# A one-core graph and expert network: building the permutation table in two matrix steps, and the order of split products in the experts

## What is computed

```python
x = x + _L0_gnn_ref(_layernorm(x), adj, ...)        # five node groups, two graph convolutions each
x = x + _L0_ffn_ref(_layernorm(x), Wg, bg, W1, b1, W2, b2)
x = x + _L1_gnn_ref(_layernorm(x), adj, nodemask, W, b)
x = x + _L1_ffn_ref(_layernorm(x), ...)             # shared MLP and 4 small experts
```

```python
gate_scores = einsum('bsd,ed->bse', x, Wg) + bg      # 8 experts
topk_scores, topk_idx = top_k(gate_scores, 2)
combine = softmax weights of the two chosen experts
for e in range(8):
    h = relu(x @ W1[e].T + b1[e])                    # 128 -> 512
    y = h @ W2[e].T + b2[e]                          # 512 -> 128
    out = out + combine[..., e:e+1] * y
```

## Time and profile before

| | us |
|---|---|
| median of 3 runs | 1334.93 (1333.78 to 1335.29) |
| the profiled execution | 1336.69 |
| its span in the trace | 1334.8 |
| block 1 | 0 to about 240.5 |
| block 2 | 240.9 to about 320.9 |
| block 3 | 321.4 to about 812 |
| block 4 | about 812 to 1334.8 |

### The profile page before, as it was taken

The page is one execution under the profiler, slowest core; times in us unless marked ns, Lnnn a source line. Parts: engine busy times, 40 slices in busy tenths (PEclk is TensorE's granted clock), DMA queues, the critical chain, the costliest instruction groups (busy, mean ns, idle before and its releaser), DMA issues. The chain is left out here.

```text
span 1334.8 us, 21838 instructions
## 1 busy us (share of the span) xinstructions
PE 1193.2 (89%) x6288; PEld 870.6 (65%) x6288; DVE 1137.0 (85%) x4033; ACT 997.9 (75%) x1947; POOL 843.4 (63%) x781
## 2 busy tenths in 40 slices
PE   5889988364999999999999993499999999999998
PEld 4767757253777777777777772366666666666665
DVE  4778998897899998999999996589898988989885
ACT  3457666493999999999999993477777777777774
POOL 3345555675777777777777763676666666667630
PEclk9999975576999999999999997599999999999999
DMA  5578764400222332322222262123222322222210
GB/s 183 200 234 265 210 184 137 169 1 19 69 80 78 78 78 78 80 79 80 79 78 79 77 77 62 54 62 85 65 70 69 84 67 70 76 76 68 68 48 24
DMA packets 137642, 124.89 MB, mean 94 GB/s; under 512 B 15630, under 2 KB 117106, under 8 KB 136371
## 3 DMA queue, kind: packets, MB, share of 16 engines
q1 hardware_dynamic: 119219, 88.06, 21.4%
q0 software_dynamic: 18304, 35.44, 11.8%
HBM read 83.78 MB, written 39.67 MB: 92 GB/s over the span
## 5 line engine op out<-in xcount | busy, mean ns | idle before, releaser
L1069 POOL DMA_INDIRECT exg<-xln_scratch,eidx x284 | 315.2, 1110 | 124.3 <-issue 69.3
L1362 POOL DMA_INDIRECT yg<-expert_rows_scratch,idx x256 | 253.4, 990 | 95.2 <-issue 72.5
L1208 DVE TENSOR_TENSOR ehl<-ehr,ehh 128x512 fp32r<-128x512 f32 x284 | 194.7, 686 | 28.7 <-ACT ehh L1093 28.5
L1090 ACT ACTIVATE ehr<-p_eh,bc 128x512 f32<-128x512 f32 x284 | 195.9, 690 | 25.1 <-PE p_eh L1128 17.0
L1093 ACT ACTIVATE ehh<-ehr 128x512 fp32r<-128x512 f32 x284 | 179.6, 633 | 9.0
L1369 POOL TENSOR_TENSOR root_l<-pre_l,mhalf 128x4 f32<-128x4 f32 x64 | 66.6, 1041 | 96.9 <-DVE pre_l L1649 96.2
L1126 PE MATMUL p_ey<-ehh,wh 128*128 128x512 f32 x284 | 124.8, 439 | 1.0 <-DVE ehl L1208 0.8
L1126 PE MATMUL p_eh<-exh,wh 128*128 128x512 f32 x284 | 124.0, 437 | 1.5 <-DVE exl L1203 1.5
L1128 PE MATMUL p_eh<-exh,wl 128*128 128x512 f32 x284 | 112.6, 396 | 0.0
L1127 PE MATMUL p_eh<-exl,wh 128*128 128x512 f32 x284 | 112.2, 395 | 0.0
L1128 PE MATMUL p_ey<-ehh,wl 128*128 128x512 f32 x284 | 111.9, 394 | 0.0
(11 more groups left out here) (228 smaller groups left out, 3152.8 us busy)
## 6 DMA issues: line engine op xcount, KB each, us to landing
expert_rows_scratch<-eyo SPq DMA_DIRECT2D x71, 256.0 KB, 2.3
xtok<-in_x_tok SPq DMA_DIRECT2D x8, 1024.0 KB, 6.8
an<-in_a_t SPq DMA_DIRECT2D x16, 512.0 KB, 4.5
xln_scratch<-xl SPq DMA_DIRECT2D x16, 512.0 KB, 4.3
at<-in_a_t SPq DMA_DIRECT2D x32, 256.0 KB, 3.0
out<-outx SPq DMA_DIRECT2D x32, 256.0 KB, 2.6
wj<-in_w_grp SPq DMA_DIRECT2D x16, 321.0 KB, 4.5
exg<-xln_scratch,eidx POOLq DMA_INDIRECT x284
```

The lines of the kernel that those rows point to most:

```text
L1069: pool.indirect_dma_start(out=xg[p][:, k, :], out_offset=None, in_=xln_d, in_offset=bass.IndirectOffsetOnAxis(ap=idx[p][:, k:k + 1], axis=0))\
L1090: nc.scalar.activation(hr[c % 2][:, :], p_h[c][:, :], ACT.Relu, bias=bc[p][:, c:c + 1])\
L1208: nc.vector.tensor_tensor(hl[:, c, :], hr[c % 2][:, :], hh[:, c, :].bitcast(F32), ALU.subtract)\
L1362: pool.indirect_dma_start(out=yg[p][:, c, k, :], out_offset=None, in_=y_d, in_offset=bass.IndirectOffsetOnAxis(ap=idx[p][:, c, k:k + 1], a ...
```

## The change

It has three parts.

1. **Start of block 1.** `cf` is loaded in two pieces: the identity first, where all of `cf` was loaded, and the rest behind the loads of the second batch. POOL and PE wait for the identity alone. The softmax of the fusion weights moves on DVE from ahead of the first turn into it, behind `pre` and `nz`.
2. **Block 2.** All 128 token columns go one way, in 16 groups of 8, by two matrix steps. The 128 tokens of a column that go to one expert have positions that lie within two neighbouring columns of the table, of which one has an even number and one an odd. First step: the weights are `mt`, 32 columns wide (2 token columns x 2 parities x 8 experts), holding the token's code; the moving matrix is the one-hot `lc` of `lo`; 16 matmuls a group fill `p_rows`, 128 rows (2 x 2 x 8 x 4) by 128. Second step: ACT copies `p_rows` to `rows_`, and one matmul with a one-hot `oh` (which row goes to which of the 284 columns, made by ACT ahead of time) adds it to `p_id`. The start column of each row comes from running counts (`p_win`, `bq`, `neg_win`), eight small matmuls and a few short DVE operations. The base of an expert enters `p_rank` by a third matmul, so `posf` is gone. The one-hot of `hi` on DVE, the scatter through memory and the last addition are gone. `lo` is stored twice in a row (`lo2`), and `lc` is now written with the 128 values innermost.
3. **Block 3.** In `up` and `down` the product with the low part of the data comes last, and the wait for it stands before that matmul; the first matmul waits only for the high part.

```diff
-TA = 2
-SC = 16
-MB = (B - SC) // TB
+MB = B // TB
+AHEAD = 5
...
-                    sp.dma_start(cf[:, :], cf_d).then_inc(c_loaded, 16)
+                    sp.dma_start(cf[:, CF_ID:CF_ID + P], cf_d[:, CF_ID:CF_ID + P]).then_inc(id_loaded, 16)
                     sp.dma_start(fw[:, :], fus).then_inc(c_loaded, 16)
                     load(1)
+                    sp.dma_start(cf[:, CF_ID + P:CF_W], cf_d[:, CF_ID + P:CF_W]).then_inc(rest_loaded, 16)
...
-                    pool.wait_ge(c_loaded, 32)
+                    pool.wait_ge(id_loaded, 16)
...
+                            if t == 0:
+                                fusion()
...
-                    for t in range(SC):
-                        for k in range(2):
-                            pool.indirect_dma_start(
-                                out=tab_d, out_offset=bass.IndirectOffsetOnAxis(ap=slot[:, k, t:t + 1], axis=0),
-                                in_=idc[:, t:t + 1], in_offset=None).then_inc(scattered, 16)
...
+                    for m in range(MB):
+                        act.wait_ge(rows_done, m + 1)
                         if m >= 2:
+                            act.wait_ge(id_done, m - 1)
+                        nc.scalar.activation(rows_[m % 2][:, :], p_rows[m % 2][:, 0:P], ACT.Copy)\
+                          .then_inc(rows_ready, 1)
+                        if m + AHEAD < MB:
+                            hot(m + AHEAD)
...
                     for m in range(MB):
                         pe.wait_ge(hot_ready, m + 1)
+                        for j in range(4):
+                            for h in range(2):
+                                for k in range(2):
+                                    last = nc.tensor.matmul(p_rows[m % 2][32 * j:32 * j + 32, 0:P],
+                                                            mt[:, k, m * TB // 2 + j, h, :],
+                                                            lc[m % 2][:, k, 2 * j + h, :],
+                                                            start=(h == 0 and k == 0), stop=(h == 1 and k == 1))
+                        last.then_inc(rows_done, 1)
+                        if m >= 1:
+                            place(m - 1)
...
                         if m >= 2:
-                            dve.wait_ge(hot_used, m - 1)
+                            dve.wait_ge(rows_done, m - 1)
                         for k in range(2):
-                            nc.vector.tensor_tensor(lc[m % 2][:, k, :, :], iota_l[:, :, :],
-                                                    lo_h[:, k, TB * m:TB * m + TB].unsqueeze(1)
-                                                    .to_broadcast([P, P, TB]), ALU.is_equal)
-                        for t in range(TB - TA):
-                            b = TB * m + t
-                            for k in range(2):
-                                last = nc.vector.tensor_scalar(hh[m % 2][:, t, k, :], iota_c, hi_f[:, k, b:b + 1],
-                                                               cf[:, CF_C + b:CF_C + b + 1], ALU.is_equal, ALU.mult)
+                            last = nc.vector.tensor_tensor(
+                                lc[m % 2][:, k, :, :].rearrange("p t (a d) -> p t a d", d=2),
+                                iota.unsqueeze(1).to_broadcast([P, TB, P // 2, 2]),
+                                lo2[:, k, TB * m:TB * m + TB, :].unsqueeze(2).to_broadcast([P, TB, P // 2, 2]),
+                                ALU.is_equal)
                         last.then_inc(hot_ready, 1)
...
                     def down(j, p, c):
+                        pe.wait_ge(hh_ready, HC * j + c + 1)
+                        nc.tensor.matmul(p_y[p][:, :], wh[p][:, cols2(c)], hh[:, c, :], start=c == 0, stop=False)
+                        nc.tensor.matmul(p_y[p][:, :], wl[p][:, cols2(c)], hh[:, c, :], start=False, stop=False)
                         pe.wait_ge(hl_ready, HC * j + c + 3)
-                        last = parts(p_y[p][:, :], wh[p][:, cols2(c)], wl[p][:, cols2(c)], hh[:, c, :], hl[:, c, :],
-                                     c == 0, c == HC - 1)
+                        last = nc.tensor.matmul(p_y[p][:, :], wh[p][:, cols2(c)], hl[:, c, :],
+                                                start=False, stop=c == HC - 1)
```

More of the change, by code:

```diff
@@ new lines, in _, with distance @@
+                    for k in range(2):
+                        for h in range(2):
+                            last = nc.scalar.activation(mt[:, k, :, h, 2 * E0 * (1 - h):2 * E0 * (1 - h) + 2 * E0],
+                                                        zero, ACT.Copy, scale=0.0)
+                    last.then_inc(pad_ready, 1)
+                    def distance(m):
+                        nc.scalar.activation(gap[m % 2][:, :], ch[:, CH_H:CH_H + NCOL], ACT.Abs,
+                                             bias=neg_win[:, m:m + 1]).then_inc(gap_ready, 1)
@@ new lines, in hot @@
+                    def hot(m):
+                        act.wait_ge(gap_ready, m + 1)
+                        last = nc.scalar.activation(oh[:, m, :], gap[m % 2][:, :], ACT.Relu, scale=-1.0, bias=1.0)
+                        if m + 2 < MB:
+                            last.then_inc(gap_used, 1)
+                            act.wait_ge(gap_used, m + 1)
+                            distance(m + 2)
+                    act.wait_ge(win_ready, 1)
+                    for m in range(2):
+                        distance(m)
@@ L870, in _ @@
+                    for m in range(AHEAD):
+                        hot(m)
                     for m in range(MB):
+                        act.wait_ge(rows_done, m + 1)
                         if m >= 2:
-                            act.wait_ge(act_hot, m - 1)
-                        for t in range(TA):
-                            b = TB * m + TB - TA + t
-                            for k in range(2):
-                                last = nc.scalar.activation(gap[m % 2][:, t, k, :], ch[:, CH_H:CH_H + NCOL], ACT.Abs,
-                                                            bias=neg_hi[:, k, b:b + 1])
@@ L896, in _ @@
                     pe.wait_ge(tot_ready, 1)
-                    nc.tensor.matmul(p_cnt[:, 0:E0], ones16, tot[:, :], start=True, stop=True).then_inc(cnt_done, 1)
+                    nc.tensor.matmul(p_cnt[:, 0:E0], ones16, totx[:, 0, 0:E0], start=True, stop=True)\
+                      .then_inc(cnt_done, 1)
+                    earlier = ch[:, CH_U:CH_U + P].rearrange("p (m t) -> p t m", t=TB)
+                    for j in range(4):
+                        for h in range(2):
+                            last = nc.tensor.matmul(p_win[32 * j:32 * j + 32, :], totx[:, h, :], earlier[:, 2 * j + h, :],
+                                                    start=(h == 0), stop=(h == 1))
@@ L906, in _, with place @@
+                    def place(m):
+                        pe.wait_ge(rows_ready, m + 1)
+                        nc.tensor.matmul(p_id[:, 0:NCOL], rows_[m % 2][:, :], oh[:, m, :],
+                                         start=(m == 0), stop=(m == MB - 1)).then_inc(id_done, 1)
+                    pe.wait_ge(pad_ready, 1)
                     for m in range(MB):
                         pe.wait_ge(hot_ready, m + 1)
[L908 to L913 removed]
@@ L950, in _ @@
[L950 to L957 removed]
+                    step(nc.vector.tensor_reduce(bq[:, :], bsel[:, :], AX.X, ALU.add))
@@ new lines, in _ @@
+                    nc.vector.tensor_tensor(val[:, 1, :, :], mask[1][:, :, :], code, ALU.mult)
+                    for k in range(2):
+                        for h in range(2):
+                            b = slice(h * B // 2, (h + 1) * B // 2)
+                            if k == 0:
+                                dve.wait_ge(rank_done, h + 1)
+                            last = nc.vector.tensor_tensor(wide[:, b, :], mask[k][:, b, :], p_rank[h][:, :, :], ALU.mult)
+                        step(last)
@@ new lines, in _, with part, half_ @@
+                    step(nc.vector.tensor_copy(par[:, :, :], par_i[:, :, :]))
+                    def part(k, c, w):
+                        a = slice(c * B // 4, (c + 1) * B // 4)
+                        return [mt[:, k, a, h, 2 * E0 * h + E0 * w:2 * E0 * h + E0 * w + E0] for h in range(2)]
+                    def half_(x, k, c, h):
+                        return x[:, k, c * B // 2:(c + 1) * B // 2].rearrange("p (i h) -> p h i", h=2)[:, h, :]
+                    iota = ch[:, CH_I:CH_I + P].rearrange("p (a d) -> p a d", d=2)
```

238 lines of the change are left out of this document (118 added, 120 removed).

## The result

The changed kernel takes 1274.18 us (median of 4 runs, 1271.83 to 1278.62) against 1335.11 for the kernel before (4 runs, 1333.78 to 1338.93): ratio 0.954, 95% interval 0.952 to 0.956. That is 61 us less; 1281 was forecast, with a range of 1271 to 1300. The profiled executions are 64.9 apart (spans 1334.8 and 1269.9), since the profiled one of after lies 2.4 under the median of its four and that of before 1.6 over the median beside it.

A forecast was written before the change was run, and what follows sets the result against it. Block 1 starts as a mostly waiting chain, DVE bounds block 2, a DVE-PE chain sets block 3's turn. Gains of 1.6 + 32 + 20 = 53.6 us from the median of 1334.93 gave 1281 us, range 1271 to 1300.

The forecast's parts named there:

- Part 1, the start: Start of block 1: POOL's power starts at 8.2 to 8.5 instead of 9.99, gaining 1.6 us (0 to 2.0), kept to the block's end.
- Part 2, the preparation: Block 2 before its loop: added and removed work sum to -0.5 us, so the loop starts at 258, give or take 2.
- Part 2, the loop: Block 2's table loop: 16 groups at 1.7 us each, 27.2, plus 1.2; part of block 2's gain of 32 us.
- the price of a narrow matmul: PE in block 2's loop: 0.112 or 0.061 us each; costly but not fatal, 1300 to 1335, chance 0.04.
- the one at 1.28 a group: Block 2's best end: all groups at 1.28 us and everything hidden, a gain of 36 us.
- The second set of `mt`: Block 2's loop: interrupts DVE and adds 1.2 us.
- The tail: End of block 2, DVE from `tge` to the last step: 4.38 us as before, putting `ids` at 288.9.
- Part 3: Block 3: the low product moves behind the others, PE sets a turn of 6.42 instead of 6.71 us, gaining 20 us.
- POOL can't follow: Block 3 rival: POOL becomes the bound, part 3 gives nothing or 11 us, time 1290 to 1301; chance 0.14.
- `lc` at one element a cycle: Block 2 loop rival: a group takes 2.46 us, block 2 gains 17, time 1296; chance 0.09.
- Slower: Block 2 loop rival: narrow matmuls don't pipeline and mode changes drain PE, over 5.0 us a group, over 1335; chance 0.03.
- The lower clock: Block 2's loop: the clock stays at 1.2 GHz, time 1286, counted inside the forecast.

The follow-up runs named there:

- part3_alone: The kernel before with the changed order of the split products in block 3 alone: 1316.60 us, ratio 0.9871.
- no_part3: The changed kernel with the old order of the split products in block 3: 1293.48 us.

## Where the prediction was right and where not

**Part 1, the start: right.** 1.6 was forecast, and the runs give about 2. The power came at 8.12, a little ahead of the 8.2 to 8.5 that was said, since `cf` was there at 4.41. That block 1 keeps the gain to its end holds on average; its own swing of 232 to 241 was not in the forecast at all, though it is larger than the term. The terms of the trace with part 1 at 2 add up to 58.2 (2 + 38.9 - 2.1 + 19.7 - 0.3), so some 3 of the 61 between the medians may be this swing, and 7 of the 64.9 between the profiled executions.

**Part 2, the preparation: right.** From the first `p_tot` to the first product 16.6 us passed; 258 was 17.1 after it. POOL's power took 21.65 us and was hidden, as in the kernel before, where it took 21.25: the 12.50 of the earlier trace rows are only the part of it in that stretch.

**Part 2, the loop: wrong by 7.5 us.** Forecast were 28.4 us (16 x 1.7 + 1.2), measured 20.9 (248.80 to 269.70). The step that failed is the price of a narrow matmul: I took the row of 0.079 as a floor and the columns as the price, 1.26 to 1.8 for sixteen. The columns were right for one strip (0.107 apart at 0.50), but the sixteen go to four strips that work side by side, and the next matmul could start 0.41 after the first of them. The Trainium skill (TensorEngine Tiling (Array Packing), section Key Properties) states both that tiles run in parallel and that a change of mode drains the engine. I kept the first out of the sum; the runs bear it out, at about four times. They agree with the second too, at 0.13 to 0.18 us a change, for which a group of 1.20 had room. The form of the sum, "1.28 + 1.26 + some 0.4 of signalling for two groups", was sound: a buffer's round of filling and emptying serves two groups. With the measured 0.65 and two `lc` of 0.61 it gives (1.22 + 0.65 + 0.4) / 2 = 1.14 a group, less than DVE's own two `lc`, so DVE set it. Of the ends that I gave, the one at 1.28 a group was the right one, and the block's gain of 38.9 lies beyond even its 36. The second set of `mt` cost 2.3, not 1.2: eight operations of 0.29, which I had priced at 2.4 in the preparation and at half of it here, and DVE had no cover for them (`p_rows` 3.48 after the one before, in place of 1.20). The tail was right (4.37 for 4.38), though it began only 0.8 ahead of PE's end and not 1.9. So `ids` came 41.1 after the block's start where 48 was forecast.

**Part 3: the mechanism and the size right, the long turns left out.** The steady turn became 6.41 for a forecast 6.42, by the mechanism named: no wait for `ehl`, starts 0.23 apart. But the 19.7 came out of 0.306 x 70 = 21.4 (the middle turn went from 6.715 to 6.409) less 1.8 that longer turns took (mean over middle turn, 2.0 us before and 3.8 after), and that the forecast of 20 lies so near is in part luck: the fall of a turn was put 0.016 too small, 1.1 us in 70, and the longer turns took back 1.8. The rival's condition, that POOL can't follow, did not come: it kept up at 6.41 and even at 6.25. What did come is a thinner lead. For the middle tile rows landed 2.6 us ahead of PE before and 1.6 after, so that late ones could be felt more. The rival's price was 9 to 20; this took about 2. The 449.9 of 450 without a wait for PE could not tell: POOL shows no such wait at 6.71, at 6.41 or at 6.25.

**The start of block 3: not in the forecast.** I put it at nothing without a reason, and it is 2.1 us, of which 2.0 are the second tile's matmuls at the lower clock. `part3_alone` shows that the new order has a share in it (21.7 for 20.2), and `no_part3` that the table has one (21.0). Why the clock rises later there I can't say.

**The rivals.** `lc` at one element a cycle did not come, for the reason given (pairs side by side); taking the pair away brought it. Slower: the change of mode that it feared shows, at a fifth of a microsecond and less. The lower clock came for the whole of the table's loop and cost nothing, since DVE held it. The price of a narrow matmul was rightly named as what could break the number, but only by being higher, and it was lower. The sign was right, and so was the mechanism but for that one price. The total was 7 us too high: 6.9 more from block 2 and some 3 that are the swing of block 1, less 2.1 at the start of block 3.

## What to carry to other kernels

When two engines hand two buffers to each other, a group costs the longest of three: the one engine's work, the other's, and half of a buffer's round. Here it was DVE's own, and all rested on the price put on the other engine. Take that price from starts, one after the other, and measure it if no row has the form. When a wait is taken away from a loop whose engines are all nearly full, an engine that never waits is not thereby the bound: look at how long ahead of its consumer its data land, and lighten the suspects apart and together. And compare blocks between traces rather than ends: here a block that the change hardly touched moved by 7 us by itself, and one profiled pair would have credited it to the change.

## What the runs showed of the hardware

- Sixteen matmuls with 32-column weights and 128 moving columns take 0.44 us over four strips and 1.06 in one, at a granted clock of 1.00; 0.65 and 1.91 at 0.50. By starts they hold PE for 0.24 and 0.90, and for 0.41 and 1.71. The order (strip by strip, or changing each time) makes no difference. One strip costs as much as full width. A full-width matmul behind narrow ones starts 0.13 us later than a narrow one would at 1.00.
- An equality of two 16-bit operands, 1,024 elements on a partition, takes 0.61 us if the repeated operand lies twice in a row in memory, 1.15 if one stored value is repeated in place.
- Twenty dense matmuls of 512 columns brought the granted clock to 1.00 before a block; 1 us after a wait of 2.52 us (and another of 1.25 before it) it was back at 0.50.
- A POOL that gathers four times 128 rows a turn never waited for PE at turns of 6.71, 6.41 and 6.25 us and kept up in all three; with three gathers it waits 1.7 us of 6.4. The rows landed 1.6 us behind the end of the last issue for the middle tile, and up to 6.1 at the end of the block. Its index copy of 128x4 took 0.34 us in the mean, 0.18 where it came after a wait.
